# Second attention in tiles of two tokens: scores of a batch in four half banks, heads regrouped by DMA, block transposes on VectorE

## What is computed

```
def _L0_xattn_ref(q, k, v, Wq, bq, Wk, bk, Wv, bv, Wo, bo):
    Q = (q @ Wq.T + bq).reshape(bs, sl, H, HD)
    K = (k @ Wk.T + bk).reshape(bs, sl, H, HD)
    V = (v @ Wv.T + bv).reshape(bs, sl, H, HD)
    score = jnp.einsum('bshd,bsgd->bshg', Q, K)
    weight = jax.nn.softmax(score, axis=-1)
    attn = jnp.einsum('bshg,bsgd->bshd', weight, V).reshape(bs, sl, nf)
    return attn @ Wo.T + bo
```

## Time and profile before

| | us |
|---|---|
| median of 3 runs (2190.33 to 2190.97) | 2190.4 |
| the profiled execution | 2188.47 |
| its span, first to last instruction | 2186.8 |
| PE busy in the span (93%) | 2029.5 |
| DVE, ACT, POOL busy | 1134.3, 772.3, 269.1 |

### The profile page before, as it was taken

How to read it: one execution, slowest core, us unless ns; L and a number is a source line. 1 busy time by engine, 2 the same in 40 slices (tenths; PEclk the granted TensorE clock), 3 DMA queues, 4 the chain that set the end, 5 groups by cost and what they waited for, 6 DMA issues and landing times.

```text
span 2186.8 us, 33859 instructions
## 1 busy us (share of the span) xinstructions
PE 2029.5 (93%) x12432; PEld 1634.0 (75%) x12432; DVE 1134.3 (52%) x1948; ACT 772.3 (35%) x2035; POOL 269.1 (12%) x234
## 2 busy tenths in 40 slices
PE   5999993888888879999999999999999999999997
PEld 5777773787777766777777777777777777777776
DVE  4555555355555544455636455454555454554655
ACT  5466562333333323243323223232232332322321
POOL 3343344122112220000000000000000000000000
PEclk9999996899999979999999999999999999999999
DMA  2000002211121102020301102002020030200011
GB/s 82 28 31 19 29 20 92 47 42 43 44 47 41 35 1 83 1 80 12 96 6 39 50 12 79 9 26 60 11 75 11 6 81 11 75 11 6 12 44 39
DMA packets 66401, 84.00 MB, mean 38 GB/s; under 512 B 10256, under 2 KB 43152, under 8 KB 65560
## 3 DMA queue, kind: packets, MB, share of 16 engines
q1 hardware_dynamic: 66336, 83.12, 13.3%
HBM read 64.58 MB, written 5.77 MB: 32 GB/s over the span
## 4 chain that ended last, share of the span: by engine, by line
PE 59%; issue 1%; DVE 1%; ACT 1%; POOLq 0%; POOL 0%; DVEq 0%
PE pair L1682 10%; PE pair L1684 10%; PE pair L1683 10%; PE y_ps L1682 3%; PE y_ps L1683 3%; PE qa_ps L1682 3%; PE y_ps L1684 3%; PE qa_ps L1683 2%; PE qa_ps L1684 2%; PE pair L1804 2%; PE pair L1805 2%; PE qd_ps L1851 1%; PE pair L1766 1%; PE qd_ps L1852 1%; PE qd_ps L1683 1%
## 5 line engine op out<-in xcount | busy, mean ns | idle before, releaser
L1682 PE MATMUL pair<-XH,GUH 128*128 128x512 f32 (+1 forms) x960 | 375.9, 392 | 0.0
L1684 PE MATMUL pair<-XH,GUL 128*128 128x512 f32 (+1 forms) x960 | 375.5, 391 | 0.0
L1683 PE MATMUL pair<-XL,GUH 128*128 128x512 f32 (+1 forms) x960 | 374.7, 390 | 0.0
L1596 DVE TENSOR_TENSOR h<-pair,sg 128x512 f32<-128x512 f32 (+1 forms) x120 | 82.8, 690 | 422.8 <-ACT sg L1384 422.7
L1384 ACT ACTIVATE sg<-pair 128x512 f32<-128x512 f32 (+1 forms) x120 | 71.7, 597 | 474.4 <-PE pair L1805 381.2
L1684 PEld LDWEIGHTS pair<-XH,GUL 128*128 128x128 f32 (+1 forms) x960 | 171.7, 179 | 47.7
L1683 PEld LDWEIGHTS pair<-XL,GUH 128*128 128x128 f32 (+1 forms) x960 | 171.8, 179 | 47.4
L1682 PEld LDWEIGHTS pair<-XH,GUH 128*128 128x128 f32 (+1 forms) x960 | 171.6, 179 | 47.1
L1286 POOL TENSOR_TENSOR qb_raw<-qb_raw,qb_scale 128x704 f32<-128x704 f32 x8 | 13.7, 1707 | 1063.5 <-DMA qb_scale<-in_gu_scale 1063.5
L1296 ACT ACTIVATE XH<-xe 128x512 fp32r<-128x512 f32 x128 | 78.8, 633 | 179.1 <-DVE xe L1618 179.1
L262 ACT ACTIVATE p<-s_ps,nm 128x128 f32<-128x128 f32 (+1 forms) x256 | 103.8, 429 | 76.5 <-DVE nm L345 76.5
(11 more groups left out here) (295 smaller groups left out, 4580.8 us busy)
## 6 DMA issues: line engine op xcount, KB each, us to landing
gu_raw<-in_gu SPq DMA_DIRECT2D x20, 512.0 KB, 4.0
wrep<-soft_f SPq DMA_DIRECT2D x64, 128.0 KB
dw_raw<-in_dw SPq DMA_DIRECT2D x10, 512.0 KB, 3.8
xT_raw<-in_xT SPq DMA_DIRECT2D x8, 512.0 KB, 3.8
x_raw<-in_x SPq DMA_DIRECT2D x8, 512.0 KB, 3.5
c_raw<-in_cT SPq DMA_DIRECT2D x8, 512.0 KB, 4.4
KS<-fmk SPq DMA_DIRECT2D x64, 64.0 KB, 2.1
QS<-fmv SPq DMA_DIRECT2D x64, 64.0 KB, 2.1
```

Of the source, the lines that this page charges most:

```text
L1596: nc.vector.tensor_tensor(h[0:M, b, :], pair[b][1][0:M, :], sg[0:M, b, :], ALU.mult).then_inc(h_rdy, 1)
L1682: mm(out, wh, xh, start=first, stop=False)
L1683: mm(out, wh, xl, start=False, stop=False)
L1684: return mm(out, wl, xh, start=False, stop=last)
```

## The change

`cross` gets another layout for everything between the projections and the output projection.

- Two tokens (t and t+128) make a tile: 2 x 16 heads = 32 rows and 32 columns. The 128 partitions hold four groups g of 32 tokens of either half. `scores(b)` is 128 fp32 matmuls of 32 x 32 x 32 in one go for the whole batch, each on one diagonal block of the array, into the halves of four banks (`so_ps`). The operands are read at a step of 32 elements. The blocks of different tokens are first set to -1e30 by four matmuls of 256 columns with a constant (`apart`). The scores are once a batch, not eight times.
- Softmax once a batch on 128 x 1024: DVE maxima, DVE subtraction into `pr`, one ACT exponential, DVE sums, DVE reciprocals, POOL `divide`.
- DVE turns probabilities and values in 32 x 32 blocks (`probs_turned`, `values_turned`); the PE transposes, `QG`, `QS`, `KS`, `VG` and the copies for them are gone. `values(b)` is again 128 matmuls of 32 x 32 x 32, into the other halves of the four banks.
- SP moves keys, values and queries of a batch with 16 DMAs each (`by_token`, 32 partitions x 2 x 128 elements), and a new move of 16 DMAs takes the attention's result back (`by_head`): 64 a batch and not 24. Projections use three banks, the context and the queries' input have split copies of their own (CH, CL and XH, XL), loaded and split two batches ahead.
- The constants of POOL are eight small fills in place of fills of 8 x 1024 and 8 x 4096.

The core of the diff (line numbers of the kernel before stand in the section above):

```diff
-        KS, QG = sb("KS", [ROWS, 2, NH, P]), sb("QG", [ROWS, 2, 4, P])
...
+        apart_f, apart, identR = sb("apart_f", [P, 8, 2, NH]), sb("apart", [P, 8, 2, NH], F32R), sb("xidentR", [P, P], F32R)
...
-            nc.gpsimd.memset(QG[:], 0.0).then_inc(consts, 1)
-            nc.gpsimd.memset(KS[:], 0.0).then_inc(consts, 1)
-            pool.wait_ge(consts, 3)
-            nc.gpsimd.memset(KS[0:8, :, :, :], NEG).then_inc(consts, 1)
-            pool.wait_ge(consts, 4)
-            for part, fill in ((QG[0:8, :, :, :].rearrange("p s a (h t) -> p (s a h) t", t=8), 1.0),
-                               (KS[0:8, :, :, :].rearrange("p s h (a t) -> p (s h a) t", t=8), 0.0)):
-                nc.gpsimd.affine_select(out=part, in_=part, compare_op=ALU.not_equal, fill=fill, base=0,
-                                        pattern=[[0, part.shape[1]], [1, 8]], channel_multiplier=-1).then_inc(consts, 1)
+            nc.gpsimd.memset(apart_f[:], 0.0).then_inc(consts, 1)
+            pool.wait_ge(consts, 2)
+            for r in range(0, P, 32):
+                for u in range(2):
+                    part = apart_f[r:r + 32, :, u, :]
+                    nc.gpsimd.affine_select(out=part, in_=part, compare_op=ALU.is_ge, fill=NEG, base=(15, -16)[u],
+                                            pattern=[[0, 8], [0, NH]], channel_multiplier=(-1, 1)[u]).then_inc(consts, 1)
...
+        FM = [sb(f"fm{n}", [P, 2, 4, KC, 32]) for n in "qkv"]
+        TM = [sb(f"tm{n}", [P, 2, NH, 32]) for n in "qkv"]
+        OT, OM = sb("ot", [P, 2, NH, 32]), sb("om", [P, 2, 4, KC, 32])
+        VT = sb("xVT", [P, 32, HD])
+        pr, PT = sb("pr", [P, 4, 8, 32]), sb("xPT", [P, 4, 8, 32])
...
+        so_ps = ctx.enter_context(nc.psum_tensor("so_ps", [P, 4, 512], F32))
+        j_ps = [ctx.enter_context(nc.psum_tensor(f"xj_ps{i}", [P, 512], F32)) for i in range(3)]
+        t_ps = ctx.enter_context(nc.psum_tensor("xt_ps", [P, 4, P], F32))
+        scores_of = so_ps[:, :, 0:S].rearrange("p k (m g) -> p k m g", g=32)
...
+        MOVED = 16 * 16
...
+            def by_token(to, fm, landed):
+                for j in range(4):
+                    for g in range(4):
+                        sp.dma_start(to[32 * g:32 * g + 32, :, 4 * j:4 * j + 4, :].rearrange("p s c t -> p s (c t)"),
+                                     fm[32 * j:32 * j + 32, :, g, :, :].rearrange("p s c t -> p s (c t)")).then_inc(landed, 16)
+            def by_head():
+                for j in range(4):
+                    for g in range(4):
+                        sp.dma_start(OM[32 * j:32 * j + 32, :, g, :, :].rearrange("p s c t -> p s (c t)"),
+                                     OT[32 * g:32 * g + 32, :, 4 * j:4 * j + 4, :].rearrange("p s c t -> p s (c t)")).then_inc(l_ot, 16)
...
-                for rows, to, fm, ready, landed in ((0, KS, FM[1], k_rdy, l_ks), (HD, QS, FM[2], v_rdy, l_vs),
-                                                    (0, QS, FM[0], q_rdy, l_qs)):
-                    sp.wait_ge(ready, KC * (b + 1))
-                    for j in range(4):
-                        sp.dma_start(to[rows:rows + HD, slot, j:NH:4, :],
-                                     fm[HD * j:HD * j + HD, :, slot * P:slot * P + P]).then_inc(landed[slot], 16)
...
+                after(sp, s_done, b)
+                alone(sp, past)
+                by_token(TM[1], FM[1], l_kt)
...
             def batch(b, first, last):
                 if not last:
-                    context(b + 1)
-                stack(b, 1)
+                    keys_moved(b + 1)
+                sp.wait_ge(ot_rdy, 2 * (b + 1))
+                alone(sp, past)
+                after(sp, ol_rdy, 2 * b)
+                alone(sp, past)
+                by_head()
                 if not last:
-                    stack(b + 1, 0)
-            over_batches(sp, batch)
+                    values_moved(b + 1)
+                    queries_moved(b + 1)
+            def body(b, first, last):
+                if not last and not (isinstance(b, int) and b == B - 2):
+                    context(b + 2)
+                batch(b, first, last)
+            body(0, True, False)
+            with sp.Fori(1, B - 2) as b:
+                body(b, False, False)
+            body(B - 2, False, False)
+            body(B - 1, False, True)
...
+            def divide(b):
+                pool.wait_ge(rinv_rdy, b + 1)
+                nc.gpsimd.tensor_tensor(pr[:], pr[:], rinv[:].unsqueeze(3).to_broadcast([P, 4, 8, 32]),
                                         ALU.mult).then_inc(norm_rdy, 1)
...
+            def exps(b):
+                act.wait_ge(sub_rdy, b + 1)
+                nc.scalar.activation(pr[:], pr[:], ACT.Exp).then_inc(exp_done, 1)
+            def heads_out(b, s):
+                if s == 0:
+                    act.wait_ge(o_done, b + 1)
+                    after(act, l_ot, MOVED * b)
+                copy(OT[:, s].rearrange("p h (k m) -> p k m h", k=4),
+                     so_ps[:, :, S:2 * S].rearrange("p k (m u h) -> p k m u h", u=2, h=NH)[:, :, :, s, :]).then_inc(ot_rdy, 1)
+            def o_high(b, s):
+                act.wait_ge(l_ot, MOVED * (b + 1))
+                after(act, wo_done, 2 * (b - 1) + s + 1)
+                copy(OH[:, s].rearrange("p c (g t) -> p c g t", g=4), OM[:, s].rearrange("p g c t -> p c g t")).then_inc(oh_rdy, 1)
...
+            def values_turned(b):
+                dve.wait_ge(l_vt, MOVED * (b + 1))
+                after(dve, o_done, b)
+                nc.vector.transpose(VT[:], TM[2][:].rearrange("p s h t -> p t (s h)")).then_inc(vt_rdy, 1)
+            def less_maxima(b):
+                dve.wait_ge(s_done, b + 1)
+                nc.vector.tensor_reduce(top[:], scores_of, AX_X, ALU.max).then_inc(max_rdy, 1)
+                dve.wait_ge(max_rdy, b + 1)
+                sub(pr[:], scores_of, top[:].unsqueeze(3).to_broadcast([P, 4, 8, 32])).then_inc(sub_rdy, 1)
+            def reciprocals(b):
+                dve.wait_ge(exp_done, b + 1)
+                nc.vector.tensor_reduce(sums[:], pr[:], AX_X, ALU.add).then_inc(sum_rdy, 1)
+                dve.wait_ge(sum_rdy, b + 1)
+                nc.vector.reciprocal(rinv[:], sums[:]).then_inc(rinv_rdy, 1)
+            def probs_turned(b):
+                dve.wait_ge(norm_rdy, b + 1)
+                nc.vector.transpose(PT[:], pr[:]).then_inc(pt_rdy, 1)
...
+                less_maxima(b)
+                if not last:
+                    keys_out(b + 1, 0)
+                    keys_out(b + 1, 1)
+                if not first:
+                    norm_out(b - 1, 0)
+                    norm_out(b - 1, 1)
+                reciprocals(b)
+                if not last:
+                    keys_out(b + 1, 2)
+                    keys_out(b + 1, 3)
+                if not first:
+                    features_out(b - 1, 0)
+                probs_turned(b)
+                if not first:
+                    features_out(b - 1, 1)
+                if not last and not (isinstance(b, int) and b == B - 2):
+                    context_low(b + 2)
+                if not last:
+                    queries_out(b + 1, 0)
+                    queries_out(b + 1, 1)
+                o_low(b, 0)
+                o_low(b, 1)
+                if not last:
+                    queries_out(b + 1, 2)
+                    queries_out(b + 1, 3)
+                    values_turned(b + 1)
+                if not last and not (isinstance(b, int) and b == B - 2):
+                    x_low(b + 2)
+                residual(b, 0, own)
+                residual(b, 1, own)
+                own.close()
...
+            def by_pairs(one):
+                for m in range(8):
+                    for n in range(4):
+                        for g in range(4):
+                            done = one(m, (n + g) % 4, slice(32 * g, 32 * g + 32))
+                return done
+            def scores(b):
+                after(pe, sub_rdy, b)
+                for k in range(4):
+                    mm(so_ps[:, k, 0:S], identR[:], apart[:].rearrange("p m u h -> p (m u h)"), start=True, stop=False,
+                       skip_group_check=True)
+                pe.wait_ge(l_kt, MOVED * (b + 1))
+                pe.wait_ge(l_qt, MOVED * (b + 1))
+                alone(pe, past)
+                def one(m, k, rows):
+                    t = 8 * k + m
+                    return mm(so_ps[rows, k, 32 * m:32 * m + 32], TM[0][rows, :, :, t].rearrange("p s h -> p (s h)"),
+                              TM[1][rows, :, :, t].rearrange("p s h -> p (s h)"), start=False, stop=True, skip_group_check=True)
+                by_pairs(one).then_inc(s_done, 1)
+            def values(b):
+                pe.wait_ge(pt_rdy, b + 1)
+                pe.wait_ge(vt_rdy, b + 1)
+                after(pe, ot_rdy, 2 * b)
+                alone(pe, past)
+                def one(m, k, rows):
+                    at = S + 32 * m
```

(22 more changed lines are left out.)

371 lines of the change are left out of this document (123 added, 248 removed).

## The result

The changed kernel takes **2219.9 us** (median, 2218.6 to 2222.4), against 2190.4 before: a ratio of 1.0136, 95% interval 1.0119 to 1.0154. The forecast was 2220.0. The profiled execution took 2219.6 us with a span of 2217.8. Of the 31 us that the span grew, 28 lie in `cross`: it ended at 849, before at 820.7. Its last split ended at 359.2, before at 368.2, and PE's first projection started at 362.8, before at 371.2. So the stage started its work 8.5 us earlier and ended 28 us later.

What follows compares the result with a forecast made beforehand. SP's issues, in a ring with PE through `cross`, were taken as the bound: 404.9 + 7 x 56.5 - 1.0 + 47.5 = 846.9 against 820.7, +26.2, and +4 for slow issues; 2188.5 + 30 = 2218.7, median 2220 us, range 2205 to 2240.

Steps and rivals of the forecast that it cites:

- slow issues, apart: In `cross`, some SP issues take a microsecond more, and 512 moves come with more unrolled code: +4 us.
- the ring: Scores wait for queries issued last; next keys wait for projection after scores: 14.4 + 40.6 + 1.5 = 56.5 us a batch.
- The issue: SP's time for one 32 x 2 x 128 move, taken as 601 ns from the nearest row; the other end is 387.
- the rival with 0.30: Shorter middle dimension makes SP's issue shorter: some 2162 us at 0.52 from issue to issue, 2122 at 0.43; chance 0.30.
- From scores to keys: From scores' start, through keys' projection and DVE's copies, to SP's start on the next keys: 14.4 us, scores 4.6.
- First batches: First batch in `cross` takes 1.0 us less than the 56.5 us ring, having no norm_out in it.
- Start of the stage: Small POOL fills end before DVE's split, main block starts 7.9 us earlier; first moves lose that and 5.5 us more.
- End of the stage: After the last scores no projection hides anything; from there to the end of `cross` takes 47.5 us.
- The rule on issuing: Skill's rule of small issue time would shrink 40.6 us to four landings; forecast said it fails for moves this small.
- The dear small matmuls: Rival: PE's small matmuls read at a step of 32 elements take 53 ns each, 9.1 us more a batch, 2293 us; chance 0.11.
- The tight ring: Rival: clock up and small matmuls at 12 ns take 3.7 us off each of 7 batches, 2194 us; chance 0.07.

Runs made afterwards that it cites:

- the run with 716 instructions: Against the kernel with mask and score matmuls done twice: projections and output projection cut to one product, half the values' small matmuls replaced by four; 2241.2 us.
- The written-out loop: Against the changed kernel: TensorE's loop over the batches written out so each batch's instructions run once, other engines keep their loops; 2247.7 us (ratio 1.0278).
- the kernel with two issuing engines: Against the changed kernel: half of each move's 16 DMAs issued from ScalarE's queue, half by SP, order unchanged; 2113.1 us (ratio 0.9651).
- the last two kernels: Changed kernel with queries' move first and half the DMAs on ScalarE: result conversion before its queries' half, 2119.6 us; then also x_high and residuals earlier, 2093.7 us.
- at 952: Against the changed kernel: mask matmuls and all 128 score matmuls of a batch done twice into the same banks; 2317.9 us.

## Why the prediction was right

It named the mechanism. That the time came out within 0.1 us of the forecast is luck: the first two batches took 9 us more than it had for them, and the steady ones together 9 us less.

| step | forecast | measured |
|---|---|---|
| first keys' move | 372.9 | 371.8 |
| first scores | 404.9 | 404.6 |
| first to third scores | 2 x 56.5 - 1.0 = 112.0 | 121.4 |
| third to last scores | 5 x 56.5 = 282.5 | 273.0 |
| first to last scores | 394.5 | 394.3 |
| last scores to the end of the stage | 47.5 | 49.9 |
| slow issues, apart | 4 | in the rows above |
| end of the stage | 850.9 | 848.9 |
| span | 2217 (2218.7 - 1.7) | 2217.8 |

- **What sets the ring.** Right, and shown from three sides: added issues lengthen it one for one, a group taken out of it shortens it, and so do halved groups. Also right were the order of the queue as the cause, that the result is ready before its move's turn (1.5 us to spare, 2.7 in the forecast), and that PE stands idle before the scores. SP's wait for the keys is 13.1 us, where the forecast had 16.
- **The issue.** Taken at 0.601 us, 0.635 from one to the next; measured 597 ns, 10.2 for 16. The choice of the nearest row (same kind of memory at both ends, same partitions) was right. The 387 ns that carried the rival with 0.30 came from a DMA out of DRAM, and no SBUF form tried here came below 561. The chance of 0.30 was too much for a row of another kind.
- **From scores to keys.** 14.4 forecast, 11.7 measured. The scores took 3.9 and not 4.6. The forecast explained its 18 ns an instruction by the low clock; measured are 15 ns for the scores at either level of the clock, 12 for the values at 1.00, and 14 for the values at 0.54. The low clock lasted 2 us into the keys, not 5.3: the earlier trace rows showed a clock's rise after a long idle time, and here PE had already worked for 3.8 us. (That PE on small matmuls alone doesn't raise the clock, as the forecast had it, is not so in the run with 716 instructions: 0.50 in the first 256, 0.96 in the next.) The two norm_out took 0.5 us less. The gaps between SP's groups gave 1 us back. So the steady ring was 1.9 us too long in the forecast.
- **First batches.** From the first scores to the third it is 121.4 us (404.64 to 525.99), 12 more than two steady batches; the forecast had 4 for the whole stage, added at its end. It looked only at SP's slow issues; TensorE's own pauses of 1.4 to 2.4 us in its small matmuls were missed, and so was that SP's issues stretch at the same time (11.6 and 11.7 us for 16). The written-out loop carries the same slowness through all batches, with fetches in them; steady batches of the changed kernel have neither.
- **Start of the stage.** The shorter fills gave the 7.9 us, and a little more: the last split ended 9.0 us earlier and the first projection started 8.5 us earlier. A long fill put back costs 6.5 us by the medians.
- **End of the stage.** 2.4 us over, by pauses in the last batch's small matmuls, 1.0 in the scores and 1.8 in the values, whose code is run once:

```profile
802.36 1.81 PE L1011 MATMUL so_ps<-tmk,tmq 32*32 32x32 f32 x106 [1.02 <-issue]
...
816.85 1.81 PE L1023 MATMUL so_ps<-xPT,xVT 32*32 32x32 f32 x116 [1.81 <-issue]
```

- **The rule on issuing.** Two queues issue at once without slowing each other (597 and 624 ns), but one issue takes a third of the 1.9 us to landing here (rows below), and a batch has 64 of them: saving half of it was worth 107 us. The Trainium skill, "DMA: Bandwidth & Descriptors", section "Issuing engines are not separate DMA queues", says that several issuing engines only save the time to initiate a DMA, and calls that time usually small relative to the DMA. The first half agrees with these runs; the second doesn't hold for moves of 32 KB. The result's move in the changed kernel:

```profile
L661 SPq DMA_DIRECT2D om<-ot x128: 585/597/1315, 431.7 to 830.7; - x128
...
DMA to landing us min/median/max: 1.9/1.9/2.8
```

- **The dear small matmuls.** The rival with 0.11 asked for 53 ns an instruction and is refuted by 12 to 15. But its reason may hold in small. At a clock of 1.00 the scores' 256 instructions, which read both operands at a step of 32 elements, took 3.86 us, and the values' 256, which read them contiguously, 3.10: 0.8 us more, 3 ns each. The Trainium skill, "Advanced Engine Details and Errata", section "Memory Cachelines", says that in SBUF a different cacheline for each access costs performance, which would fit. But the scores also add to the mask where the values start anew, and in the kernel with two issuing engines the values took 3.9 to 4.1 us at a clock of 1.00, and in the last two kernels the scores took 4.0 to 4.6; no run separates these. On VectorE the transpose that reads at a step of 32 takes 1.90 us and the contiguous one of the same size 1.23, likewise untested.
- **The tight ring.** The third rival, 0.07, was cheap to doubt and rightly small. Its 3.7 us a batch were the clock's, and the clock is worth 0.9, since it leaves the scores' time as it is.

## What to carry to other kernels

When a queue issues DMAs in a ring with the compute engines, count issues and not bytes, and look at which of them stand between the last producer and the first consumer: a group moved behind the one that is waited for gained 83 us here without one instruction fewer. An engine that issues is an engine that works: when you spread issues over engines, put every conversion and eviction that somebody waits for ahead of them, or the gain is lost (51 us a batch against some 38 with the same work). And count a loop's instructions before you add to it.

## What the runs showed of the hardware

- Issuing a move from SBUF to SBUF costs SP 561 to 678 ns in the five forms tried, from 32 x 128 to 128 x 2 x 128 elements; ScalarE takes 624, at the same time as SP.
- Instructions are fetched again where a pass of TensorE's loop is long: at 716 matmul instructions not (46 packets in the execution), at 952 in each pass (97 packets), with pauses of 0.4 to 1.9 us in the rows shown. In the written-out loop pauses come in each batch, and SP's 16 issues take 11.2 to 11.7 us instead of 10.2.
- 256 matmul instructions of 32 x 32 x 32 on four diagonal blocks took 3.1 us at a clock of 1.00 and 3.6 at 0.54 with contiguous reads; with reads at a step of 32 elements, and adding to what stands there, 3.9 at both 1.00 and 0.50. In the kernels with two issuing engines the first kind took up to 4.1 and the second up to 4.6 at 1.00, for a reason that no run shows. The granted clock fell from 1.00 to 0.50 in the middle of them in one run, while PE was not idle in them, and stood at 1.00 through all of them in another.
- A VectorE split of 128 x 2048 takes 9.43 us beside a GpSimd affine_select of 8 x 4096, and 2.29 without. Beside memsets of the same size it took 2.29.
